# A two-layer perceiver block: the first unit's key rows go out ahead of the other keys, and one engine issues all their loads

## The reference

```python
x = x + cross_attention_0(norm(x), ctx)      # 16 heads of 8, 2048 context rows per batch, mask added
x = x + causal_latent_attention(norm(x))     # over the 128 tokens
x = x + norm(x) @ W[idx] + b[idx]            # idx drawn by logits and a given noise
x = x + cross_attention_1(norm(x), ctx)      # the same context, other weights
x = x + self_attention(norm(x))
x = x + mixture_of_experts(norm(x))          # 16 experts of 64, 4 chosen per token, and 2 shared
```

```python
k = ctx @ wk; v = ctx @ wv; q = norm(x) @ wq / sqrt(8)
attn = softmax(q @ k.T + mask) @ v           # 128 queries x 2048 keys
```

## Time and profile before

| | |
|---|---|
| median of three runs | 305.71 us (305.68 to 336.32) |
| profiled execution | 305.52 us, of which 303.5 us are the span shown in the profile |
| TensorE busy | 284.2 us (94% of the span) |
| VectorE, ScalarE, GpSimd busy | 227.0, 206.4, 68.7 us |
| mean clock granted to TensorE | 0.989 of full speed |
| moved by DMA | 28.06 MB |

### The profile page before, as it was taken

How to read it: one execution, slowest core, us unless ns; L and a number is a source line. 1 busy time by engine, 2 the same in 40 slices (tenths; PEclk the granted TensorE clock), 3 DMA queues, 4 the chain that set the end, 5 groups by cost and what they waited for, 6 DMA issues and landing times.

```text
span 303.5 us, 10281 instructions
## 1 busy us (share of the span) xinstructions
PE 284.2 (94%) x4324; PEld 185.0 (61%) x4329; DVE 227.0 (75%) x371; ACT 206.4 (68%) x436; POOL 68.7 (23%) x135
## 2 busy tenths in 40 slices
PE   7957999999999999899989899999999999999995
PEld 5444666667676664453745567666666765436575
DVE  6944889999999983563638999999999970643583
ACT  5656689898998987524433698998989987133350
POOL 6793500110101003520000676001011021110001
PEclk9996999999999999999999999999999999999999
DMA  7973415532222450333100025522221100000000
GB/s 229 409 282 123 158 55 171 184 102 77 80 80 82 139 217 2 121 140 104 55 2 0 3 65 181 176 81 82 71 83 60 56 3 2 0 2 3 0 0 19
DMA packets 10898, 28.06 MB, mean 92 GB/s; under 512 B 2241, under 2 KB 3329, under 8 KB 10466
## 3 DMA queue, kind: packets, MB, share of 16 engines
q1 hardware_dynamic: 10776, 27.16, 26.6%
q10 hardware_dynamic: 74, 0.20, 0.2%
HBM read 20.74 MB, written 6.62 MB: 90 GB/s over the span
## 4 chain that ended last, share of the span: by engine, by line
PE 71%; DVE 15%; DMA 5%; ACT 3%; POOL 2%; issue 2%; SPq 1%; ACTq 1%; DVEq 0%; POOLq 0%
PE bank L1040 70%; DVE mx L812 10%; DMA ctxT_s<-in_ctxT 2%; DMA k_first_rows<-kparts 2%; DMA kpair<-k_first_rows 1%; ACT probs L545 1%; DVE s_neg L867 1%; POOL m_rows L427 1%; DVE negm L819 1%; ACTq L276 1%; DVE st L723 1%; DVE kparts L782 0%; PE bank L1336 0%; DVE k_rest L779 0%; POOL m_rows L429 0%
## 5 line engine op out<-in xcount | busy, mean ns | idle before, releaser
L812 DVE TENSOR_REDUCE mx<-bank 128x2 f32<-128x1024 f32 x128 | 153.0, 1222 | 16.1 <-PE bank L1040 12.7
L545 ACT ACTIVATE probs<-bank 128x512 f32<-128x512 f32 x256 | 139.3, 595 | 20.1 <-PE bank L1040 16.1
L1040 PE MATMUL bank<-q_exp,kpair 64*128 64x128 bf16 x1024 | 84.7, 218 | 1.9 <-ACT probs L545 1.2
L1040 PE MATMUL bank<-probs,v_all 128*9 128x128 f32 x2048 | 80.3, 274 | 1.1 <-ACT probs L545 1.0
L1040 PE MATMUL bank<-kpair,q_rows 64*128 64x512 bf16 x256 | 73.7, 387 | 5.6 <-DMA kpair<-k_first_rows 5.1
L1040 PEld LDWEIGHTS bank<-q_exp,kpair 64*128 64x128 bf16 x1024 | 55.3, 94 | 31.6 <-issue 12.7
L1040 PEld LDWEIGHTS bank<-probs,v_all 128*9 128x9 f32 x2048 | 43.2, 90 | 16.7 <-ACT probs L545 4.0
L427 POOL CAST m_rows<-negm 128x2 bf16<-128x2 f32 x32 | 6.9, 217 | 144.6 <-DVE negm L819 144.6
L1040 PEld LDWEIGHTS bank<-kpair,q_rows 64*128 64x128 bf16 x256 | 22.7, 93 | 7.4 <-issue 5.5
L482 ACT ACTIVATE v_all<-bank 128x512 f32<-128x512 f32 (+1 forms) x20 | 10.5, 539 | 13.3 <-PE bank L1040 13.3
L1040 PE MATMUL bank<-selq,ident_b 128*128 128x512 bf16 x70 | 17.8, 379 | 0.3
(11 more groups left out here) (219 smaller groups left out, 341.9 us busy)
## 6 DMA issues: line engine op xcount, KB each, us to landing
k_scratch<-kparts SPq DMA_DIRECT2D x24, 256.0 KB, 2.9
kpair<-k_scratch SPq DMA_DIRECT2D x62, 96.0 KB
kpair<-k_scratch SPq DMA_DIRECT2D x62, 64.0 KB
ctxT_s<-in_ctxT SPq DMA_DIRECT2D x4, 512.0 KB, 6.0
mask_s<-in_mask SPq DMA_DIRECT2D x2, 1024.0 KB, 10.3
kpair<-k_scratch SPq DMA_DIRECT2D x62, 32.0 KB
wM<-in_packM SPq DMA_DIRECT2D x1, 1728.0 KB, 7.0
wB<-in_packB SPq DMA_DIRECT2D x1, 599.0 KB, 5.0
```

The source lines that it names most:

```text
L545: act.activation(probs[:, j % 4, :], bank[:, 4 + j % 2, :], ACT.Exp).then_inc(S("exp_done"), 1)
L812: V.tensor_reduce(mx[n % 2][:, w, :], bank[:, 2 * (w % 2):2 * (w % 2) + 2, :], AX.X, ALU.max) \
L1040: return T.matmul(out_, lhsT=lhsT, rhs=rhs, start=start, stop=stop, **kw)
```

## The change

`k_first_rows` is stored ahead of the first half's `store_k` and no longer behind it. The second half's `store_k(0, 0, 1)`, which stood between that store and the wait for it, goes behind the loads of unit 0. ScalarE's two waits and three DMAs are taken out, and SyncE issues all six loads of unit 0.

```diff
-        def first_head(eng, a):
+        def first_head(a):
...
-                eng.dma_start(kpair[0][row:row + times * HD, :], src).then_inc(S("k_loaded0"), 16)
+                nc.sync.dma_start(kpair[0][row:row + times * HD, :], src).then_inc(S("k_loaded0"), 16)
...
-            store_k(0, 0, 0)
             sp.wait_ge(S("k_low"), 4)
             sp.dma_start(kfirst, kparts[0:2 * HD, :, 0:SK]).then_inc(S("k_first"), 16)
-            store_k(0, 0, 1)
+            store_k(0, 0, 0)
             sp.wait_ge(S("k_first"), 16)
             sp.wait_ge(S("k_ones"), U)
-            first_head(sp, 0)
+            for a in range(2):
+                first_head(a)
+            store_k(0, 0, 1)
             cross_k(0, 1)
...
-            act.wait_ge(S("k_ones"), U)
-            act.wait_ge(S("k_first"), 16)
-            first_head(act, 1)
             for k in range(2):
                 put_rows(0, k)
```

## The result

| | before | after |
|---|---|---|
| median | 305.96 us (305.68 to 336.32, 4 runs) | 310.34 us (309.11 to 312.32, 4 runs) |
| ratio | 1 | 1.0149, interval 1.0109 to 1.0190 |
| profiled execution, span | 305.52, 303.5 us | 310.05, 308.0 us |
| mean granted clock | 0.989 | 0.983 |

The run of 336.32 us is a slow one and stands outside the ratio. The change costs 4.4 us by these medians, and the forecast was 307.6, at most 309.4.

The account below looks back on a forecast made before the run. TensorE was taken to bound the kernel, with one long stall of 5.11 us for unit 0's loads. 305.52 + 0.5 (unit 1 late) + 1.4 (second clock fall) gave 307.4 us profiled, 307.6 median, range 304.8 to 309.4.

Parts of the forecast that it names:

- What bounds: Whole kernel: TensorE, busy 94% of the span; its one long stall, 5.11 us, awaits unit 0's loads; unit 1 is next.
- Part 1: Store of the first rows: without the first half's store ahead, 1.99 us sooner, landing at 16.9 us.
- Part 2: Unit 0's six loads by SyncE alone: issued in 3.9 us; TensorE starts at 22.95, 2.07 us earlier.
- Part 3: ScalarE without its three issues (2.34 us): copies end by 21.6; worth up to 1.0 us at unit 0, already counted.
- Part 4: Second half's store behind the loads: unit 1 taken up at 31.65 against 31.14, 0.5 us later, after a 2.6 us wait.
- Part 5: SyncE behind unit 1: `wB`, `wC` and unit 2 move by 3.8 us but stay hidden, costing nothing.
- Part 6: TensorE's clock: a second fall to half, in the stall at unit 1, costs 1.4 us, at most 1.85.
- rival B: Stall at unit 1 as forecast, but the clock holds there or recovers before the loop: 306.2 us, chance 0.27.
- the likeliest case: Stall at unit 1 replaces half of unit 0's and the clock falls again: 307.6 us, 306.7 to 308.6, chance 0.42.
- The sum: Whole kernel: 305.52 + 0.5 + 1.4 = 307.4 us for a profiled execution, 307.6 as median.
- Rival E: First rows bound by something other than the queue ahead; unit 0 starts as before, unit 1 late: 309.5 us, chance 0.03.
- D: First rows land no earlier than 18.9, or SyncE's loads land slowly; 1.7 to 2.0 us later: 309.5 us, chance 0.12.

Follow-up runs that it names:

- parts apart: Changed kernel with the first rows' store as three DMAs, one per part, read from three groups of 16 partitions: 311.21 us, ratio 1.0155.
- the kernel filled without branch: Changed kernel with unused matmuls ahead of TensorE's waits for units 0 and 1, and without its mask branch: 308.13 us, ratio 1.0070.
- those two kernels: Changed kernel with the first rows' store as three DMAs, from one group of 16 partitions (311.41 us, 1.0140) or from three (311.21 us, 1.0155).

## Why the prediction was wrong

**What bounds (right).** Unit 1's keys, and not unit 0's, decide the changed kernel. With unit 1's wait removed the loss is gone; with unit 0 started earlier (parts apart) it stays.

**Part 1, the step that failed.** The prediction took 1.99 us of stores off the 4.82 us, which leaves 2.83. The store took 4.29, 1.46 us more. It had two bounds: the queue ahead of it, and its own slow reading of 16 partitions. Taking away the first uncovered the second. Here are the stretches behind its issue at 15.33 in the changed kernel:

```profile
15.50:16.00 0.50, 0.50 (x6) 0.50 (x6) 0.50 (x1) 0.21 (x2) 0.50 (x1) 1.00 0.04 16
16.00:16.50 0.50, 0.50 (x7) 0.50 (x5) 0.50 (x2) 0.47 (x1) 0.42 (x2) 1.00 0.04 16
```

Hardly anything moves until 16.5; then the engines are busy until 18.5 at 97 GB/s on average, about the store's 197 thousand bytes, and it lands at 19.62. At the 395 GB/s by which the prediction reckoned, the same bytes would move in 0.5 us and not 2.0. That difference of 1.5 us is about the size of the error. What stands behind the store may have a part in it, as said above.

The range had 18.9 as upper end, and 19.62 is beyond it because of the second error, in the same step: the issue, at 14.07 in both kernels by the prediction, was at 15.33. Over the profiles it lies from 14.07 to 15.47, by how fast TensorE gets through the first projections: four 512-column matmuls took 2.77 us in the changed kernel's profile, and 1.94 before. With the old order the full queue absorbed this, as the three landings near 18.9 show; in the new order each such delay goes through to unit 1. That TensorE's clock at the start makes the delay is argued only: the record of the clock does not show it there.

The Trainium skill's page "SBUF — State Buffer" (Door 1) says that a DMA's speed depends on how many of 16 ports its partitions reach, four partitions in a row sharing one, and those 32 further on sharing it too. By it 16 partitions reach 4 ports of 16. An estimate from the 435 GB/s that the Trainium skill's page "DMA: Bandwidth & Descriptors" (Specifications) states for all 16 is 109 GB/s. The traces agree in the main. From 16 partitions it was 111 GB/s from 17 to 18 us in the changed kernel, and 78 in the same stretch of the kernel filled without branch. From the 32 partitions of two units it was 201, and from 48 it was 193, each from 16 to 17 us; by the Trainium skill's table of ports there 48 reach 8 ports, as 32 do. The three places do not test the page cleanly, as the stretch with 180 GB/s may be mixed.

**Part 2 (right).** Six loads by SyncE took 3.97 us for 3.9, and from the first of them to TensorE it was 25.76 - 19.64 = 6.12 us for 6.00. Unit 0 started late only by part 1.

**Part 3 (right in itself).** ScalarE was done at 21.2, and nothing came of it.

**Part 4 (right but for its start).** From the store's issue to unit 1's first load it was 28.69 - 23.66 = 5.03 us for 4.85, from there to TensorE 5.81 for 5.90. TensorE took unit 1 up at 34.50 for 31.65: 1.26 for the late issue, 1.46 for the store's own time, 0.13 for the rest.

**Part 5 (right).** Neither `wC` nor unit 2 was waited for.

**Part 6 (right in size for a short fall, too narrow).** 1.4 us was forecast for the second fall of the clock, at most 1.85, and 1.47 measured between two profiles of the same kernel. It falls in some runs only, as rival B has it; the likeliest case and B are one kernel's two ways. A third way was not foreseen: the long fall of some 10 us, with a mean clock of 0.972, which costs about 3.4 us by the estimate above. The changed kernel's own highest runs, 312.32 and 311.48 us, have mean clocks of 0.973 and 0.972, as those two kernels have.

**The sum.** 34.50 - 31.14 = 3.36 us at unit 1, and 1.47 for the clock, make 4.83; the spans differ by 4.5, and where the other 0.3 us are won back was not looked for. The forecast had 0.5 and 1.4. Rival E named the cause (the first rows are bound by something other than the queue ahead of them) and D its effect (no earlier than 18.9, 1.7 to 2.0 us on every later time of SyncE). Both gave 309.5, and their chances, 0.03 and 0.12, were too low.

## What to carry to other kernels

A transfer that is late in a full queue has its own time under that cover: find out how fast it is alone, above all when it reads few partitions (16 here), before taking off what stands ahead of it. An early start for the first consumer is worth nothing if the second one's data moves back by more; move the wait itself (here: two units in the early store) rather than the store. And a full queue can absorb jitter that a tighter order passes on.

## What was not expected of the hardware

- All 16 DMA engines were busy and moved 111 GB/s, from 16 partitions, and 201 from 32: twice the bytes in the same 4.3 us from issue to landing.
- Behind a branch TensorE's first instruction came at 25.95 though its data was there at 20.40; without the branch (and the code of its other way) at 21.21. Where TensorE waits for keys until 24 or 25 anyway it costs nothing that was measured.
- The clock fell 2.0 us after TensorE stopped in the profile before, and more than 4 us after (20.3 to behind 24.5) in the one after. In these two, how long TensorE had stood still does not tell when the clock falls. And the second fall lasted from 34.8 to 38.2 in one profile and from about 35 to behind 45 in two others.
- SyncE's six loads took from 3.97 to 6.14 us to issue in kernels that differ in nothing ahead of them, and 3.97 and 4.57 in two profiles of the same kernel. Why was not found.
